# Attention and FFN layer on one core: x statistics one slot sooner, P's copies ahead of the results, x's low parts last in the next k projection, and moves in the last slots

## The reference, cut to what matters

```python
x = x + layernorm(attn(layernorm(x)))        # x is (8, 512, 1024): 8 rows of 512 tokens
x = x + layernorm(ffn(layernorm(x)))
# attn: qkv = x @ w_qkv.T + b; 8 heads of 64; scores = k . q, causal with -10000 where masked,
#       softmax over the key axis, vals = attn . v, then vals @ w_o.T + b_o
# ffn:  x @ W.T + b, plus a low-rank product x @ A[:r].T @ B[:, :r].T whose rank r is routed by
#       an argmax over four gate scores
```

## Time and profile before

| | us |
|---|---|
| median of 3 timed runs (lowest to highest) | 1476.23 (1475.44 to 1476.61) |
| the profiled execution, its own time | 1475.65 |
| span of the trace (first to last instruction) | 1473.7 |
| PE busy | 1452.9 (99%) |
| PEld busy | 1286.1 (87%) |
| DVE busy | 922.2 (63%) |
| ACT busy | 696.1 (47%) |
| POOL busy | 634.2 (43%) |

### The profile page before, as it was taken

The page is one execution under the profiler, slowest core; times in us unless marked ns, Lnnn a source line. Parts: engine busy times, 40 slices in busy tenths (PEclk is TensorE's granted clock), DMA queues, the critical chain, the costliest instruction groups (busy, mean ns, idle before and its releaser), DMA issues.

```text
span 1473.7 us, 24715 instructions
## 1 busy us (share of the span) xinstructions
PE 1452.9 (99%) x7852; PEld 1286.1 (87%) x7852; DVE 922.2 (63%) x2106; ACT 696.1 (47%) x1501; POOL 634.2 (43%) x1155
## 2 busy tenths in 40 slices
PE   7999999999999999999999999999999999999997
PEld 6888888888888888888888889999999999999997
DVE  7476575675674775765855886555555555555565
ACT  6475465564573663754654763333333323333331
POOL 2253361461462452533622674444444444444442
PEclk9999999999999999999999999999999999999999
DMA  7212113112122122121122622222211122222111
GB/s 253 76 40 72 59 29 100 36 39 82 36 55 66 41 55 75 39 59 62 39 57 90 204 86 72 72 72 72 71 65 52 60 71 71 71 71 71 64 43 43
DMA packets 47073, 102.97 MB, mean 70 GB/s; under 512 B 5056, under 2 KB 21440, under 8 KB 47040
## 3 DMA queue, kind: packets, MB, share of 16 engines
q1 hardware_dynamic: 47040, 102.54, 22.3%
HBM read 60.06 MB, written 25.69 MB: 58 GB/s over the span
## 4 chain that ended last, share of the span: by engine, by line
PE 54%; issue 25%; POOL 10%; POOLq 6%; ACT 2%; DVE 1%; DMA 1%; DVEq 0%; SPq 0%; ACTq 0%
PE ps_o L1338 23%; PE ps_o L1364 12%; PE ps_s L1385 5%; PE ps_t L1405 4%; POOL x L1672 4%; PE ps_v L1255 4%; POOLq L1660 4%; PE ps_v L1256 2%; POOLq L1658 2%; POOL small L1661 2%; POOL x L1680 1%; PE ps_o L1303 1%; POOL y L1672 1%; ACT f L1815 1%; PE ps_t L1264 1%
## 5 line engine op out<-in xcount | busy, mean ns | idle before, releaser
L1917 PE MATMUL ps_f<-wagh,x2Th 128*128 128x364 f32 x768 | 255.5, 333 | 0.4 <-DVE f L1774 0.2
L1917 PE MATMUL ps_f<-wagh,x2Tl 128*128 128x364 f32 x768 | 252.6, 329 | 0.0
L1917 PE MATMUL ps_f<-wagl,x2Th 128*128 128x364 f32 x768 | 252.5, 329 | 0.0
L1338 PE MATMUL ps_o<-xTh,wh 128*128 128x512 f32 x502 | 206.3, 411 | 0.9 <-DVE wl L966 0.2
L1338 PE MATMUL ps_o<-xTh,wl 128*128 128x512 f32 x502 | 197.3, 393 | 0.0
L1338 PE MATMUL ps_o<-xTl,wh 128*128 128x512 f32 x502 | 196.3, 391 | 0.0
L1657 POOL TENSOR_TENSOR small<-small,eps 128x1 f32<-128x1 f32 x91 | 27.6, 303 | 279.6 <-DVE small L1706 279.6
L1917 PEld LDWEIGHTS ps_f<-wagh,x2Th 128*128 128x128 f32 x768 | 144.3, 188 | 2.4 <-issue 1.2
L1917 PEld LDWEIGHTS ps_f<-wagl,x2Th 128*128 128x128 f32 x768 | 144.6, 188 | 1.1
L1917 PEld LDWEIGHTS ps_f<-wagh,x2Tl 128*128 128x128 f32 x768 | 144.5, 188 | 0.0
L570 POOL TENSOR_SCALAR pr<-pr,rden 128x128 f32<-128x128 f32 (+3 forms) x256 | 133.2, 540 | 0.0
(11 more groups left out here) (199 smaller groups left out, 3438.4 us busy)
## 6 DMA issues: line engine op xcount, KB each, us to landing
kst<-kst SPq DMA_DIRECT2D x64, 256.0 KB, 3.7
xt<-in_x SPq DMA_DIRECT2D x32, 512.0 KB, 3.9
xs<-in_x SPq DMA_DIRECT2D x24, 512.0 KB, 4.4
out<-x SPq DMA_DIRECT2D x23, 512.0 KB, 3.0
valsT<-vt SPq DMA_DIRECT2D x64, 128.0 KB, 2.3
vraw<-valsT SPq DMA_DIRECT2D x32, 256.0 KB, 3.3
raw<-in_wqkvT SPq DMA_DIRECT2D x12, 512.0 KB, 5.9
wag_raw<-in_wagT SPq DMA_DIRECT2D x8, 546.0 KB, 7.7
```

The costliest lines, as they stand in the source:

```text
L1338: done = pe.matmul(ps[:, :], w[:, k, c:c + P], xT[:, k, :], start=(k == 0 and w is wh and xT is xTh), stop=(k == KD - 1 and w is wl), skip ...
L1917: last = pe.matmul(ps_f[:, g, 0:GW], a[:, k, :], w[:, k, cols], start=(k == 0 and a is xh and w is wagh), stop=False, skip_group_check=True)
```

## The change

In `body`: `layernorm_stats` of tile 1 moves to the end of slot 1, of tile 2 to slot 2, of tile 3 to the beginning of slot 3. On ACT `p_hi` of groups 0 and 1 goes ahead of `vals_lo_part` in every slot, on DVE `p_lo` of both ahead of `vals_sum`. GpSimd waits for `nm_ready` of head 5 ahead of `split_x`. The k projection of pair 0 of the next row takes high by high and low by high of all four chunks of a half, and then high by low. In `last_body`: the same order of copies and results, `k_lo(3)` ahead of `next_low(3)`, `tile_vals` of tile 1 and `q_hi`/`q_lo` of pair 3 sooner, a wait of GpSimd for `nm_ready` of head 7 ahead of `tile_residual(0)`, and on PE one chunk of the last `tile_product` behind the transposes of the tile, T(7, 2) behind the first chunk of the first FFN tile, and the masked weights behind the third instead of the second.

```diff
@@ gpsimd, body and last_body
                     if h == X_SLOT:
+                        pool.wait_ge(nm_ready, 8 * b + h + 1)
                         split_x(0, b + 1, (0, 1))
...
                     if h == 7:
+                        pool.wait_ge(nm_ready, 8 * b + h + 1)
                         tile_residual(0)
@@ vector, body
                     if 1 <= h <= 3:
-                        layernorm_stats(h - 1, b + 1)
+                        layernorm_stats(0 if h == 1 else h, b + 1)
...
-                    if h == X_SLOT:
-                        p_lo(h - 1, 0, b)
-                        vals_sum(h - 2, b)
-                        p_lo(h - 1, 1, b)
-                    elif h == BARE + 1:
-                        p_lo(h - 1, 0, b)
-                        p_lo(h - 1, 1, b)
-                        vals_sum(h - 2, b)
-                    else:
-                        if h >= 2:
-                            vals_sum(h - 2, b)
-                        if 1 <= h <= NH:
-                            for g in range(2):
-                                p_lo(h - 1, g, b)
+                    if 1 <= h <= NH:
+                        for g in range(2):
+                            p_lo(h - 1, g, b)
+                    if h >= 2:
+                        vals_sum(h - 2, b)
                     if h < BARE:
                         reciprocal(h, b)
+                    if h == 1:
+                        layernorm_stats(1, b + 1)
...
-                    if h == 3:
-                        layernorm_stats(3, b + 1)
@@ vector, last_body
                 q_lo(2, b)
-                vals_sum(1, b)
                 p_lo(2, 0, b)
                 p_lo(2, 1, b)
+                vals_sum(1, b)
                 reciprocal(3, b)
+                k_lo(3, b)
                 next_low(3)
                 tile_vals_low(0)
                 p_lo(2, 2, b)
 
                 scores_max(4, b)
-                k_lo(3, b)
+                tile_vals_low(1)
                 reciprocal(4, b)
                 p_lo(3, 0, b)
+                q_lo(3, b)
                 p_lo(3, 1, b)
-                q_lo(3, b)
                 vals_sum(2, b)
-                tile_vals_low(1)
                 p_lo(3, 2, b)
@@ scalar, body
-                    if h >= 2 and h != BARE + 1:
-                        vals_lo_part(h - 2, b)
                     if 1 <= h <= NH:
                         for g in range(2):
                             p_hi(h - 1, g, b)
-                    if h == BARE + 1:
+                    if h >= 2:
                         vals_lo_part(h - 2, b)
@@ tensor, project
-                for k in ks:
-                    if (kind, p) == ("k", 0) and not first and k in (0, 4):
-                        pe.wait_ge(x_lo_dve, 8 + 3 * b - (1 if k == 0 else 0))
-                        pe.wait_ge(x_lo_pool, 5 * b - (3 if k == 0 else 0))
-                    for w, xT in ((wh, xTh), (wh, xTl), (wl, xTh)):
+                if (kind, p) == ("k", 0) and not first:
+                    if ks[0] in (0, 4):
+                        pe.wait_ge(x_hi_act, 6 * b - (2 if ks[0] == 0 else 0))
+                    if ks[0] == 4:
+                        pe.wait_ge(x_hi_pool, 2 * b)
+                    for w, xT in ((wh, xTh), (wl, xTh), (wh, xTl)):
+                        if xT is xTl and ks[0] in (0, 4):
+                            pe.wait_ge(x_lo_dve, 8 + 3 * b - (1 if ks[0] == 0 else 0))
+                            pe.wait_ge(x_lo_pool, 5 * b - (3 if ks[0] == 0 else 0))
+                        for k in ks:
+                            done = pe.matmul(ps[:, :], w[:, k, c:c + P], xT[:, k, :], ...)
@@ tensor, the end of last_body
                 tile_product(3, 1, whole[:1])
                 masked_weights(pe, NH - 2, b)
-                tile_product(3, 1, whole[1:3])
+                tile_product(3, 1, whole[1:2])
                 values(pe, NH - 2, b)
                 transpose_tile()
+                tile_product(3, 1, whole[2:3])
-                transpose_p(NH - 1, 0, b)
-                transpose_p(NH - 1, 1, b)
+                transpose_p(pe, NH - 1, 0, b)
+                transpose_p(pe, NH - 1, 1, b)
                 tile_product(3, 1, whole[3:])
-                transpose_p(NH - 1, 2, b)
@@ output phase, tensor, ffn
-                        if first and g == 2 and k == 1:
+                        if first and g == 2 and k == 0:
+                            last_transposes(pe)
+                        if first and g == 2 and k == 2:
                             last_weights(pe)
```

More of the change, by code:

```diff
@@ L27 @@
 MASKED = -10000.0
-Programs = namedtuple("Programs", "sync gpsimd vector scalar tensor last_weights last_values", defaults=(None, None))
+Programs = namedtuple("Programs", "sync gpsimd vector scalar tensor last_transposes last_weights last_values", defaults=(None,) * 3)
 class Constants:
@@ L1160, in last_body @@
                 exps(3, b)
-                vals_lo_part(1, b)
                 p_hi(2, 0, b)
                 p_hi(2, 1, b)
+                vals_lo_part(1, b)
                 k_hi(3, b)
@@ L1167, in last_body @@
                 p_hi(2, 2, b)
+                tile_vals_high(1)
                 masked_spread(2, b)
@@ L1171, in last_body @@
                 p_hi(3, 0, b)
+                q_hi(3, b)
                 p_hi(3, 1, b)
-                q_hi(3, b)
                 vals_lo_part(2, b)
-                tile_vals_high(1)
                 p_hi(3, 2, b)
@@ L1265, in masked_weights, with transpose_p, last_transposes @@
                       start=True, stop=True).then_inc(t_full[1], 1)
+        def transpose_p(pe, h, g, b):
+            H = 8 * b + h
+            if g == 0:
+                pe.wait_ge(p_ready, H + 1)
+                if h > 0:
+                    pe.wait_ge(t_lo, 3 * H)
+            elif g == 1:
+                pe.wait_ge(wt_ready, 1 + H)
+            else:
+                pe.wait_ge(t_lo, 3 * H + 1)
+            o, n = PT_GROUP[g]
+            for i, j, at in PT_BLOCKS:
+                if o <= at < o + n:
+                    last = pe.transpose(ps_t[g % 2][:, at - o:at - o + P],
+                                        pr[:, h % 2, S_OFF[i] + j * P:S_OFF[i] + (j + 1) * P], ident[:, :])
+            last.then_inc(t_full[g % 2], 1)
+        def last_transposes(pe):
+            transpose_p(pe, NH - 1, 2, NB - 1)
         def last_weights(pe):
@@ L1331, in project @@
                 c = (kind == "k") * PART + p * P
-                for k in ks:
-                    if (kind, p) == ("k", 0) and not first and k in (0, 4):
-                        pe.wait_ge(x_lo_dve, 8 + 3 * b - (1 if k == 0 else 0))
-                        pe.wait_ge(x_lo_pool, 5 * b - (3 if k == 0 else 0))
-                    for w, xT in ((wh, xTh), (wh, xTl), (wl, xTh)):
-                        done = pe.matmul(ps[:, :], w[:, k, c:c + P], xT[:, k, :],
-                                         start=(k == 0 and w is wh and xT is xTh), stop=(k == KD - 1 and w is wl),
-                                         skip_group_check=True)
+                if (kind, p) == ("k", 0) and not first:
[8 more added lines that the diff above has]
+                        for k in ks:
+                            done = pe.matmul(ps[:, :], w[:, k, c:c + P], xT[:, k, :],
+                                             start=(k == 0 and w is wh and xT is xTh),
+                                             stop=(k == KD - 1 and xT is xTl), skip_group_check=True)
+                else:
+                    for k in ks:
+                        for w, xT in ((wh, xTh), (wh, xTl), (wl, xTh)):
+                            done = pe.matmul(ps[:, :], w[:, k, c:c + P], xT[:, k, :],
+                                             start=(k == 0 and w is wh and xT is xTh), stop=(k == KD - 1 and w is wl),
+                                             skip_group_check=True)
                 if KD - 1 in ks:
@@ L1389, in scores @@
                 last.then_inc(s_done, 1)
[L1391 to L1407, removed]
             def tile_product(n, half, ks):
@@ L1466, in body @@
                     if 1 <= h <= NH:
-                        transpose_p(h - 1, 0, b)
-                        transpose_p(h - 1, 1, b)
+                        transpose_p(pe, h - 1, 0, b)
+                        transpose_p(pe, h - 1, 1, b)
                     turns(h, 1, b)
@@ L1474, in body @@
                     if 1 <= h <= NH:
-                        transpose_p(h - 1, 2, b)
+                        transpose_p(pe, h - 1, 2, b)
             def last_body(b):
@@ L1537, in tensor @@
             last_body(NB - 1)
-        return Programs(sync, gpsimd, vector, scalar, tensor, last_weights, last_values)
+        return Programs(sync, gpsimd, vector, scalar, tensor, last_transposes, last_weights, last_values)
 def output_phase(nc, whole, x, valsT, vals_stored, ps_o, C, W, bf, out):
@@ L1875, in scalar, with tensor @@
             body(NB - 1, True)
-        def tensor(pe, last_weights, last_values):
```

(3 more changed lines are left out.)

## The result

The changed kernel takes 1480.88 us (1480.2 to 1481.56) against 1476.23 (1475.44 to 1476.61): a ratio of 1.0032 with a 95% interval of 1.0022 to 1.0042, slower by 4.65 us. The forecast was 1480.7. The profiled execution took 1481.33, with a span of 1479.4.

The account below looks back on a forecast made before the run. The prediction took a DVE, ACT and POOL chain from exps(4) to k1F to bound each pass: +0.06 + 0.64 = +0.70, seven +4.9, less 0.4, +4.5 us. Forecast 1480.7 us, range 1474.0 to 1483.0.

Parts of the forecast that it names:

- What bounds: Loop pass: the DVE, ACT and POOL chain from exps(4)'s end to k1F decides; PE stalls removed between come back at k1F.
- Statistics: Slots 2 and 3: stalls ahead of (2, 0) and T(2, 2) go, together -0.53 us a pass by slot 4.
- Copies first, slot 4: ACT, slot 4: P's copies must wait for T(3, 0), so exps(4) ends later, +0.59 us a pass.
- GpSimd's wait: Ahead of split_x: GpSimd starts 0.64 us late without a pause behind, so the chain to k1F costs +0.64 a pass.
- the first rival: Faster, 1471.4 us: GpSimd doesn't move the chain to k1F, line 766's block was worth more, ACT overlaps its idle; chance 0.13.
- k0: Pair 0's k projection, low parts last: the 0.25 us stall goes but comes back ahead of k1F, net 0.
- T(5, 0): Transposes after GpSimd's late start: PE would stand there about 0.3 us, inside the k1F wait.
- Last slots: End of the loop's last row: net -0.4 us, bounds -1.1 and +0.5, with slot 4 some +0.15.

Follow-up runs that it names:

- s4: Changed kernel with pair 0's k projection taking its three products chunk by chunk again, low-part waits ahead of a half's first chunk: 104.15 us a pass.
- e3: Changed kernel without GpSimd's loop wait for nm_ready and with slot 4's result copy first again on ScalarE: a pass 1.17 us shorter than the changed kernel's.
- s2: Kernel before with only GpSimd's loop wait for nm_ready ahead of split_x added: 104.17 us a pass.
- s1: Kernel before with only the statistics of x moved sooner: 103.55 us a pass.
- e2: Changed kernel with ScalarE's result copy of slot 4 ahead of P's copies again: a pass 0.54 us shorter than the changed kernel's.
- s3: Kernel before with only P's copies ahead of the results in every loop slot, on ScalarE and VectorE: 103.96 us a pass.
- e1: Changed kernel without GpSimd's loop wait for nm_ready ahead of split_x: a pass 0.55 us shorter than the changed kernel's.
- e4: e3 with slots 3 and 4 of the last row on VectorE and ScalarE as before the change: median 1.36 us, last row 1.00 us below e3's.

## Why the prediction was right

- **What bounds.** "A stall of PE that is taken away between these two points comes back in front of k1F": shown by s4, where k0's stall is back, k1F's is 0.3 smaller and the pass is the same. What is gained ahead of the end of `exps(4)` stays gained: that is e3. s2 and s4 add that with k0's old order a longer chain is met at k0F already.
- **Statistics.** Forecast -0.53 by slot 4 together with the copies' order. Alone: -0.01 (s1), as was expected of that run. Together, without slot 4's price (e3): -0.54.
- **Copies first, slot 4.** Forecast +0.59; `exps(4)` took 4.69 from T(3, 0) where 4.70 stood, e2 gives 0.54 back, and s3, for which -0.20 + 0.59 = +0.39 was expected, shows +0.40. Net at the end of `exps(4)`: +0.04 against +0.06.
- **GpSimd's wait.** Forecast +0.64, measured +0.61 (s2), 0.55 (e1), and 0.60 at the end of the turns. Two small misses cancel: the semaphore took 0.16 instead of 0.07 (416.64 to 416.80), and the turns took 3.58 instead of 3.67 (416.80 to 420.38). Of the 0.60 the 0.04 of `exps(4)` was there already, so the wait made the chain 0.56 longer, 0.08 less than forecast: line 769 itself had ended 0.08 sooner than worked out (414.05 against 414.09 + 0.04). The rule of the Trainium skill (SBUF — State Buffer, "Who interferes with whom") held for who blocks whom, GpSimd first by 0.15; its reading as a gain, the first rival, did not: in s2 the block is gone and the pass is 0.61 longer.
- **k0.** Forecast 0: s4 is within its interval of the changed kernel. PE did not get all of the 0.25 even for the moment, as scores(6) then waited 0.20 (0.45 idle on PEld, less the ordinary distance), which I had not named. `q_lo(3)` ended just before it.
- **T(5, 0)** waited 0.24 (0.33 idle on PEld, less the ordinary distance), forecast about 0.3.
- **Last slots.** The one term that was missed: forecast -0.4, measured +0.58 (its bound was +0.5). The forecast was +0.15 for slot 4 and -0.55 for the end. The end came as forecast (-0.52, e4 against before), but the step "mostly makes good" for slot 4 failed: its edits cost 1.00 (e3 against e4). I took the start of `scores_max(4)` as 0.8 late; it was 1.35 late (825.38 - 5.05 = 820.33 against 818.98 in the trace of before, where 5.05 is the distance of the marks at the last row's start). In the trace `k_hi(3)` began 0.57 late (819.83 - 5.05 = 814.78 against 814.21), since in slot 3 too ScalarE idles until T(2, 0), 0.45 here: the same effect that I had priced in the loop's slot 4 and had not looked for here. `next_low(3)` besides took 1.60 instead of 1.41. How the 1.00 divides among these no run shows. Against it, the loop was over by 0.5 (4.9 forecast, 4.44). So the total of 4.5 stands so near to 4.65 partly by luck, by two errors of opposite sign.

## What to carry to other kernels

When PE is busy 99%, look for the wait that closes a chain through the other engines, and price an edit by what it does to that chain. A stall of PE that is removed between the chain's start and that wait comes back there; one removed ahead of the chain's start is a gain. "The consumer sooner" is not free when the producer isn't ready: a copy that was ready and stood first costs its whole time to the next thing in order once it is put behind one that has to wait. A wait that keeps two engines out of each other's way costs its whole delay if the engine made to wait has no pause behind it, however short the block was that it removes.

## What was not expected of the hardware

A GpSimd instruction on one element (line 581) takes 0.63 to 0.64 beside a VectorE low part and 0.19 without one. That fits turns taken by whole instructions, however small. Over the thirteen profiles the first pass began anywhere from 39.79 to 41.16 us, a spread of more than twice what one of the edits does to a pass. And one landing of a DMA in the last row came late in some profiles and not in others, worth up to 1.25 us. Passes and stalls have to be compared, not times from the span's start.
